# Placing the small tiles behind the large ones, so that TensorE's tiles start at multiples of 512 bytes

## What is computed

```
x  = groupnorm(x)·w + b;  q,k,v = 1x1 conv(x)              # 32 groups
x  = out_proj(softmax(q·kᵀ/16)·v) + x                      # attention per image
t  = tokens(x);  n = layernorm(t)
q,k,v = (n + silu(n·W1)·W2)·A  (three times)               # residual MLPs
t  = t + (softmax over queries (q·kᵀ))·v·Wout
n  = layernorm(t);  f = layernorm(n)·g + b
logits = f·gate;  top 2 of 8 experts, weights from softmax
t  = t + n-stream of sum_e weight_e·(gelu(f·w1_e + b1_e)·w2_e + b2_e)
```

## The kernel before, in words

| tiles | before | after |
|---|---|---|
| `ident`, `ones`, `same_group` | 0 | 0 |
| `wh`, `wl` | 64 | 0 |
| `xn`, `xs`, `qs`, `ks`, `prob`, `pr`, `xf`, `tn`, `xfT` | 224 | 0 |
| `raw`, `us`, `vs`, `vk` | 256 | 0 |
| `xg`, `xt`, `hs` | 0 | 0 |
| `w1s1`, `w2s1` (odd steps) | 64 | 0 |
| `w1s0`, `w2s0` (even steps) | 128 | 0 |
| `pick_lo`, `pick_hi` (routing) | 320 | 256 |
| `rows` (last transposes) | 0 | 448 |

## Time and profile before

### The profile page before, as it was taken

One profiled execution on the slowest core, in us unless ns is written; L12 is line 12 of the kernel. 1 busy time (PEld: TensorE's weight loads), 2 busy tenths in 40 slices (PEclk: granted clock), 3 DMA queues, 4 the chain that ended last, 5 costly groups with the idle time before them and its releaser, 6 DMA issues.

```text
span 1253.2 us, 25051 instructions
## 1 busy us (share of the span) xinstructions
PE 1154.5 (92%) x8118; PEld 1075.5 (86%) x8119; DVE 822.1 (66%) x1883; ACT 545.5 (44%) x995; POOL 342.7 (27%) x352
## 2 busy tenths in 40 slices
PE   6999999999999999999999335999999999999993
PEld 5897998988988889989888234899999999999992
DVE  4675475954667744768436777796797678856651
ACT  2533445432435334454334313674574556644431
POOL 0010002500004300025000325355455455555440
PEclk9999999999999999999999658899999999999996
DMA  5000000200001100011000133363563547533238
GB/s 164 1 4 31 1 1 1 69 34 1 1 2 35 68 1 1 1 35 35 1 1 1 62 112 106 104 198 53 170 201 52 155 90 216 147 59 54 55 46 273
DMA packets 66207, 82.70 MB, mean 66 GB/s; under 512 B 11105, under 2 KB 56545, under 8 KB 66145
## 3 DMA queue, kind: packets, MB, share of 16 engines
q1 hardware_dynamic: 52128, 63.48, 15.6%
q0 software_dynamic: 14016, 18.37, 8.2%
HBM read 60.85 MB, written 22.02 MB: 66 GB/s over the span
## 4 chain that ended last, share of the span: by engine, by line
PE 81%; DVE 8%; DMA 4%; issue 3%; SPq 1%; ACT 1%; DVEq 1%; POOL 0%; ACTq 0%; POOLq 0%
PE ps L1545 74%; PE ps L1625 2%; DMA w1r<-in_w 2%; PE ps L1587 1%; PE ps L1835 1%; PE ps L1558 1%; DMA rows<-acc_rows 1%; DVE w2s L1466 1%; DVE hs L1512 1%; DVE one_hot L1095 1%; DVE pick_hi L1103 1%; PE ps L1578 1%; PE ps L1634 1%; PE ps L1647 1%; DVE pick_lo L1098 1%
## 5 line engine op out<-in xcount | busy, mean ns | idle before, releaser
L1545 PE MATMUL ps<-xt,w1s 128*128 128x256 f32 x1746 | 257.8, 284 | 1.5 <-DVE xt L1476 1.5
L1545 PE MATMUL ps<-w2s,hs 128*128 128x256 f32 x1728 | 251.1, 280 | 2.8 <-DVE hs L1514 2.7
L1545 PEld LDWEIGHTS ps<-xt,w1s 128*128 128x128 f32 x1746 | 227.7, 190 | 2.1 <-DVE xt L1476 1.9
L1545 PEld LDWEIGHTS ps<-w2s,hs 128*128 128x128 f32 x1728 | 223.6, 188 | 4.2 <-issue 4.1
L944 ACT ACTIVATE h<-ps,b1t 128x256 f32<-128x256 f32 x288 | 137.3, 477 | 114.0 <-PE ps L1545 79.0
L704 POOL DMA_INDIRECT acc_rows<-y_w,now_s x72 | 119.8, 1665 | 166.2 <-issue 155.1
L1512 DVE CAST hs<-h 128x256 fp32r<-128x256 f32 x288 | 91.0, 316 | 71.0 <-ACT h L944 35.9
L1514 DVE TENSOR_TENSOR hs<-h,hs 128x256 fp32r<-128x256 f32 x288 | 123.0, 427 | 9.9
L1545 PE MATMUL ps<-xs,wh 128*128 128x512 f32 x384 | 123.1, 401 | 1.5 <-issue 1.5
L586 POOL TENSOR_TENSOR tl_r<-tl_eps,minus_half 128x4 f32<-128x4 f32 x16 | 16.2, 1014 | 350.8 <-DVE tl_eps L1216 350.8
L691 POOL DMA_INDIRECT xg<-xf_rows,now_g x76 | 93.2, 1226 | 47.3 <-POOL now_g L687 34.7
(11 more groups left out here) (213 smaller groups left out, 1871.5 us busy)
## 6 DMA issues: line engine op xcount, KB each, us to landing
w1r<-in_w SPq DMA_DIRECT2D x16, 1024.0 KB, 5.1
w2r<-in_w SPq DMA_DIRECT2D x16, 1024.0 KB, 8.9
b2t<-in_b SPq DMA_DIRECT2D x36, 128.0 KB, 2.9
xn<-in_x SPq DMA_DIRECT2D x4, 1024.0 KB, 4.9
acc_rows<-r_out SPq DMA_DIRECT2D x4, 1024.0 KB, 4.5
xf_rows<-xf SPq DMA_DIRECT2D x4, 1024.0 KB, 4.9
rows<-acc_rows SPq DMA_DIRECT2D x8, 512.0 KB, 7.4
out_tokens<-cols_out SPq DMA_DIRECT2D x8, 512.0 KB, 9.0
```

The costliest lines, as they stand in the source:

```text
L1545: ins = t.matmul(out, left[l], right[r], start=first and n == 0, stop=last and n == 2, **more)
```

## The change

The declarations change their order, and two things are added. In the image stage `minus_half`, `minus_one`, the bias, row, gate and norm tiles and `spare` go behind the large tiles. In the expert stage a padding of 64 bytes, `to_512`, goes in front, and `now_g`, `now_s` and `b1t` go to the end. The instructions, their order, waits and DMAs stay as they are.

```
@@ first tiles
         same_group = sb("same_group", [P, P])
-        minus_half = sb("minus_half", [P, 8])
-        minus_one = sb("minus_one", [P, 8])
         logits = sb("logits", [P, TILES, E])
@@ image stage
         wl = bs("wl", [P, VB + 1, KC, C], F32R)
+        xn = bs("xn", [P, KC, T])
+        xs = [bs(f"xs{i}", [P, KC, T], F32R) for i in range(2)]
...
+        xf = bs("xf", [P, NT, C])
...
+        hold_tn = bs("hold_tn", [P, NT * C])
...
+        raw = sb("raw", [P, 14, KC * C], F32, here)
...
+        hold_r2 = sb("hold_r2", [P, 4096], F32, batch_scope)
+        minus_half = bs("minus_half", [P, 8])
+        minus_one = bs("minus_one", [P, 8])
         q_bias = bs("q_bias", [P, KC])
...
         gate_sb = bs("gate_sb", [P, KC, E])
-        xn = bs("xn", [P, KC, T])
...
+        spare = bs("spare", [P, 1])
         gn_bn = bs("gn_bn", [P, KC, 2, 6])
...
         tl_nb = bs("tl_nb", [P, 2, NT])
-        xf = bs("xf", [P, NT, C])
...
-        hold_r2 = sb("hold_r2", [P, 4096], F32, batch_scope)
         batch_scope.close()
@@ expert stage
+        es("to_512", [P, 16])
         xg = es("xg", [P, 2, SUB, C])
...
         y_w = es("y_w", [P, 2, SUB, C])
-        now_g = es("now_g", [P, 2, SUB], I32)
-        now_s = es("now_s", [P, 2, SUB], I32)
         w1s1 = [es(f"w1s1{i}", [P, KC, FF], F32R) for i in range(2)]
...
-        b1t = es("b1t", [P, 2, FC])
         b2t = es("b2t", [P, 2, C])
...
         w2s = ([es(f"w2s0{i}", [P, FC, C], F32R) for i in range(2)], w2s1)
+        b1t = es("b1t", [P, 2, FC])
+        now_g = es("now_g", [P, 2, SUB], I32)
+        now_s = es("now_s", [P, 2, SUB], I32)
         ex_scope.close()
```

More of the change, by code:

```diff
@@ L115, in hybrid_block_kernel @@
         wl = bs("wl", [P, VB + 1, KC, C], F32R)
+        xn = bs("xn", [P, KC, T])
+        xs = [bs(f"xs{i}", [P, KC, T], F32R) for i in range(2)]
+        qs = [bs(f"qs{i}", [P, KC, T], F32R) for i in range(2)]
+        ks = [bs(f"ks{i}", [P, KC, T], F32R) for i in range(2)]
+        tok = bs("tok", [P, NT, C])
+        prob = bs("prob", [P, 2, T])
+        pr = [bs(f"pr{i}", [P, 2, T], F32R) for i in range(2)]
+        xf = bs("xf", [P, NT, C])
+        here = ExitStack()
+        tn = sb("tn", [P, NT, C], F32, here)
+        here.close()
+        xfT = sb("xfT", [P, KC, T], F32, here)
+        here.close()
+        hold_tn = bs("hold_tn", [P, NT * C])
+        here = ExitStack()
+        raw = sb("raw", [P, 14, KC * C], F32, here)
+        raw_vo = sb("raw_vo", [P, KC * C], F32, here)
+        vb_wide = sb("vb_wide", [P, KC, P], F32, here)
+        vb_col = sb("vb_col", [P, KC], F32, here)
+        here.close()
+        us = [[sb(f"us{n}{i}", [P, KC, T], F32R, here) for i in range(2)] for n in range(2)]
+        here.close()
+        x2 = sb("x2", [P, NT, C], F32, here)
+        r_out = sb("r_out", [P, NT, C], F32, here)
+        here.close()
+        hold_r1 = sb("hold_r1", [P, 8192], F32, batch_scope)
+        vs = [sb(f"vs{i}", [P, NT, C], F32R, here) for i in range(2)]
+        here.close()
+        v32 = sb("v32", [P, NT, C], F32, here)
+        vk = [sb(f"vk{i}", [P, 2, C], F32R, here) for i in range(2)]
+        here.close()
+        hold_r2 = sb("hold_r2", [P, 4096], F32, batch_scope)
+        minus_half = bs("minus_half", [P, 8])
+        minus_one = bs("minus_one", [P, 8])
         q_bias = bs("q_bias", [P, KC])
@@ L152, in hybrid_block_kernel @@
         tl_nb = bs("tl_nb", [P, 2, NT])
[L153 to L181, removed]
         batch_scope.close()
```

## The result

The changed kernel takes 1258.9 us (median of 12 runs, 1257.21 to 1263.0); the kernel before, run beside it, 1255.3 (12 runs). The ratio is 1.0037, its interval 1.0023 to 1.005; it is one of means, 1259.3 to 1254.7, and leaves out one run of the kernel before that took 2637 us. So the changed kernel is slower by 3.6 us in the medians and by 4.6 us in the means, where 12 us less were predicted. The profiled execution is the longest of the twelve, 1263.0 us.

The account below looks back on a forecast made before the run. The prediction took the distance between TensorE matmul starts as the bound. Gains of 4.8 + 8.0 less 0.7 give 12.1 us off 1255.06, plus 0.4 to the median: 1243 us; its own range 1234 to 1252, stated overall 1226 to 1269.

Parts of the forecast that it names:

- The bound: TensorE, busy 92% of the span: how far apart two matmuls start sets the time.
- edits costed at nothing: VectorE, ScalarE, GpSimd small tiles, `rows` and routing tiles move: no cost counted, 192 small matmuls under 1 us.
- Term 1: 768 products of 512 columns with a weight as stationary side: 234.3 to 228.0 ns each, 4.8 us gained.
- floor: Streaming time taken from plain float32 products, 24 of 256 columns at half rate: 215.8 ns each.
- Term 2: 5586 products of 256 columns, in expert steps, with `pr` and with weights moving: 116.5 ns at 0 apart, 8.0 us gained.
- The give-back: Six waits on the second half of `hs` in the expert steps: up to 0.7 us of term 2 returns as longer waits.
- Rival (b): Both sides sweep the same addresses in step, so 256-column products take 121.2 ns everywhere: slower, 1269 us; chance 0.22.
- Rival (a): Equal offsets lock the best pattern in: all 256-column products at 113.3 ns, 1224 us; chance 0.10.
- Rival (c): Offsets do not set the distance, or the edit misses real 512-byte boundaries by 128 bytes: no change, 1255.4 us; chance 0.20.
- The two rules: Skill rules weighed: independent read ports would make the gain nil; 16-byte SBUF lines would leave the time at 1255.4 us.

Follow-up runs that it names:

- true_512: Changed kernel with 384 bytes of padding ahead of the first tile, so every tile starts at a real multiple of 512 bytes; 1259.91 us, one run.
- best_3: Changed kernel with padding setting distances: steps 448, `vs` 64, `vk` 32, `xs` to `wh` 64, `us` to `wh` 448; 1245.43 us, ratio 0.9942 to the kernel before.
- sweep_2: Changed kernel with padding setting distances: even expert steps 320, odd 256, `vs` 320, `vk` 448, `xs` to `wh` 64, `us` to `wh` 448; 1251.52 us, one run.
- split_hs: Changed kernel with `hs1`, the low half, alone moved by 192 bytes, all else at distance 0; 1259.48 us, one run.

## Why the prediction was wrong, point by point

**The bound** was right: the distance between two starts in one line sets the time. No wait was added, and nothing outside line 1546 shows in the difference. That the edits costed at nothing cost nothing fits the sums, which close to within 1 us in the two traces; no run took those edits alone.

**Term 1** was right. The 30 products came to 228.0 ns, the predicted number. Over all 768 the gain is 4.1 us for 4.8, as the run of 30 that gave 234.3 was slower than the mean of its kind, 233.7, and the mean after is 228.3. The 215.8 ns that the prediction calls a floor entered no sum, and no run comes down to it: the lowest mean with 512 columns is 226.9.

**Term 2 failed, and with it the forecast.** The step that failed is "the series 160, 128, 64, 32 apart reads 121.2, 118.0, 117.5, 117.1, so I take 116.5 at 0". Measured at 0: 119.6 to 120.1, so that 8.0 us of gain became 12.0 of loss. The series was no series. Its first member was mis-read (119.6 without the first distance); read rightly it falls toward 0 all the same, so the mis-reading is not what misled. Its members differ in kind of product as much as in distance, and the map shows that the values do not run evenly: 96 is slow, 64 quick, 0 slow. A value that no row shows was set by a line through its neighbours, while the only row that is 0 apart had other columns.

**The give-back** worked as described, with the sign of term 2 turned round: slower products shortened the waits, 2.7 to 1.1 us.

**Rival (b)** is what happened, at 22 in 100: 0 apart is good with 512 columns and bad with 256. Its price was too high, 121.2 for a measured 119.9 (from the same mis-read row), hence 1269 and not 1259; but its point of decision, a mean above 118.9 ns, was passed. Its own evidence, the even half slower than the odd, is true but weak: 128 is slower than 64 in the map, and 96, which is not a multiple of 128, is slower still. What spoke against it, 32 apart being quick, is true and says nothing of 0. That the two sides conflict address by address was only argued, and still is. The measured time lies inside the stated 1226 to 1269 only by this rival, not by the forecast's own 1234 to 1252.

**Rival (a)**: something did lock in, but at 120 and not at 113.3. **Rival (c)**: that the edit misses real boundaries by 128 bytes is without effect (true_512); that offsets do not count is refuted by best_3, which differs from the changed kernel by padding tiles alone and takes some 0.9% less, and by the map.

**The two rules.** The traces show the same 3474 products of the steps at 117.2 (best_3) or 119.9 ns (after) by start addresses alone. The Trainium skill, TensorE: Matmul & The Clock Gate, section "Part 2: What happens when you issue a matmul", says that loading the next weights takes no read bandwidth from the running matmul; the runs speak against this for these products, though they do not show that it is the load that is met. The Trainium skill, SBUF — State Buffer, section "Specifications (TRN2)", gives lines of 16 bytes; all distances here are multiples of 32 bytes and yet differ, so these lines do not account for what the runs show.

## What to carry to other kernels

Where TensorE issues back to back, read the distances of single starts, split by columns, and do not carry a finding with 512 columns over to 256. "Aligned" is not the same as fast: what counted here was moving start minus stationary start modulo 256 bytes, and equal offsets were the worst choice for 256 columns. A padding tile adds no instruction and is cheap to try, and a value that no row shows is to be measured, not read off a trend.

## What the runs showed of the hardware

With float32r products of 256 columns and a weight load before each, starts lie 113 to 128 ns apart, depending on distance: nearly all 119 to 121 at 0, the same at 256 in most places, a mixture elsewhere. The mixture has a memory: the same pair takes 113.3 or 117.7 according to what ran around it (sweep_2). With 512 columns the best distance is 0, 226.9 to 229.9 ns by kernel and kind, and most others give 232 to 234.

What stays open is the mechanism. The records of loads begin when the product before begins and last 188 to 194 ns, while the product that uses the load begins 110 to 120 ns later with 256 columns, and 228 later with 512. So with 256 columns a load would overlap its own product by some 70 ns, and with 512 it has ended. That fits split_hs (own pair) and that 0 apart is slow with 256 columns only, but it was argued from records, and no run took the overlap away. Nor was it tried what in the products before decides between the mixtures, or why no whole step comes below 117.0 where `wh,us` reaches 113.8.
